# Moving the next image's front work in a four-layer image kernel: statistics among score maxima, filter products in two blocks, and another order of its chain

## What is computed

```python
# L0: decoupled dynamic filter
pooled = x.mean((2, 3))
y = relu(pooled @ w1.T + b1)                       # 12 values
y = (y @ w2.T + b2).reshape(B, C, K * K)           # 9 taps a channel
y = (y - y.mean(-1)) / (y.std(-1, ddof=1) + 1e-10)
cf = y.reshape(B, C * K * K) * fn_std              # channel filter
sf = einsum('bchw,nc->bnhw', x, ws) + bs           # spatial filter, 9 taps a pixel
sf = (sf - sf.mean(taps)) / (sf.std(taps, ddof=1) + 1e-10) * GAIN / K
out = sum over the taps of  patch * cf * sf
# L1: v * sigmoid(q . mean(k))    L2: 3x3 convolution with ternary weights, and bias
# L3: softmax attention over all 3136 pixels: Q, K of 16 channels, V of 64
S = einsum('bkp,bkq->bpq', Q, K)
z = einsum('bpq,bvq->bvp', softmax(S), V)
```

## Time and profile before

| | |
|---|---|
| median of 3 runs | 1789.23 us (1788.2 to 1789.5) |
| profiled execution | 1787.96 us, its span 1786.2 us |
| busy, share of the span | PE 92%, DVE 69%, ACT 68%, POOL 62% |
| mean granted TensorE clock | 0.966 |
| HBM | 8 GB/s over the span |

### The profile page before, as it was taken

The page is one execution under the profiler, slowest core; times in us unless marked ns, Lnnn a source line. Parts: engine busy times, 40 slices in busy tenths (PEclk is TensorE's granted clock), DMA queues, the critical chain, the costliest instruction groups (busy, mean ns, idle before and its releaser), DMA issues.

```text
span 1786.2 us, 29864 instructions
## 1 busy us (share of the span) xinstructions
PE 1635.4 (92%) x10892; PEld 830.9 (47%) x10892; DVE 1239.0 (69%) x2443; ACT 1212.1 (68%) x2300; POOL 1102.3 (62%) x926
## 2 busy tenths in 40 slices
PE   5887899999988799999998979999999888999997
PEld 4464344444446344444443634444444454444442
DVE  5946777775684877777387388777748648777760
ACT  2045899988413689899732378999972337899994
POOL 2720478889751067888865016888887402788888
PEclk9988999999989999999998899999999899999998
DMA  2004000000000400000000040000000012000000
GB/s 88 1 1 90 1 6 7 7 7 6 11 1 1 90 2 6 7 7 12 6 6 1 3 88 1 6 11 7 7 6 6 0 26 29 2 11 7 7 7 11
DMA packets 12388, 26.83 MB, mean 15 GB/s; under 512 B 4560, under 2 KB 8912, under 8 KB 11728
## 3 DMA queue, kind: packets, MB, share of 16 engines
q1 hardware_dynamic: 12240, 24.92, 5.9%
HBM read 8.73 MB, written 6.42 MB: 8 GB/s over the span
## 4 chain that ended last, share of the span: by engine, by line
PE 67%; DVE 17%; ACT 8%; issue 5%; POOL 3%; POOLq 0%; DVEq 0%; ACTq 0%
PE PS L1315 25%; PE PS L1271 12%; PE PS L1241 11%; PE PS L1213 6%; DVE nmt L688 5%; PE PS L1169 3%; ACT Pb L956 3%; DVE nmt L681 3%; DVE Pb L595 3%; ACT PS L911 2%; PE PS L1128 2%; PE PS L1161 2%; PE PS L1204 1%; POOL accP L1076 1%; PE PS L1205 1%
## 5 line engine op out<-in xcount | busy, mean ns | idle before, releaser
L681 DVE TENSOR_REDUCE nmt<-PS 128x1 f32<-128x448 f32 x1176 | 681.2, 618 | 211.5 <-PE PS L1241 207.9
L1076 POOL TENSOR_TENSOR accP<-accP,Pb 128x512 f32<-128x512 f32 (+1 forms) x532 | 677.4, 1273 | 130.3 <-ACT Pb L956 82.2
L956 ACT ACTIVATE Pb<-PS 128x896 f32<-128x896 f32 (+1 forms) x700 | 636.5, 914 | 124.5 <-PE PS L1271 117.2
L1315 PE MATMUL PS<-Pb,VT 128*64 128x448 f32 x2800 | 660.9, 545 | 4.3 <-ACT Pb L956 3.6
L1241 PE MATMUL PS<-Ka,Qa 96*64 96x448 bf16 x2888 | 498.6, 356 | 23.5 <-ACT PS L911 10.7
L1271 PE MATMUL PS<-Qa,Ka 99*64 99x448 bf16 x2744 | 492.4, 354 | 3.0 <-ACT Pb L956 2.5
L911 ACT ACTIVATE PS<-PS,nmt 128x448 f32<-128x448 f32 x588 | 357.1, 607 | 33.6 <-DVE nmt L688 27.9
L1241 PEld LDWEIGHTS PS<-Ka,Qa 96*64 96x64 bf16 x2888 | 166.4, 110 | 269.6 <-issue 116.5
L1271 PEld LDWEIGHTS PS<-Qa,Ka 99*64 99x64 bf16 x2744 | 168.6, 110 | 242.1 <-issue 188.1
L1315 PEld LDWEIGHTS PS<-Pb,VT 128*64 128x64 f32 x2800 | 195.6, 137 | 104.1 <-ACT Pb L956 28.5
L834 ACT ACTIVATE xnp<-xw,nb,rstd 128x448 f32<-128x448 f32 x56 | 40.4, 749 | 195.3 <-DVE nb L503 195.3
(11 more groups left out here) (145 smaller groups left out, 1440.6 us busy)
## 6 DMA issues: line engine op xcount, KB each, us to landing
xin<-in_x SPq DMA_DIRECT2D x4, 1568.0 KB, 11.3
out<-xw SPq DMA_DIRECT2D x28, 224.0 KB, 1.9
Qa<-parts SPq DMA_DIRECT2D x24, 168.0 KB, 7.1
Ka<-parts SPq DMA_DIRECT2D x24, 112.0 KB, 4.0
Ka<-parts SPq DMA_DIRECT2D x24, 84.0 KB, 2.5
Qa<-mpt SPq DMA_DIRECT2D x96, 1.3 KB
wz<-in_weights SPq DMA_DIRECT2D x1, 829.0 KB, 7.7
Qa<-parts SPq DMA_DIRECT2D x24, 28.0 KB, 1.9
```

Of the source, the lines that this page charges most:

```text
L681: nc.vector.reduce_max(nmt[:, target % 2, b, t:t + 1], PS[0:BLK, bank, 0:CH], X, negate=True).then_inc(mx_free, 1)
L956: nc.scalar.activation(Pb[0:r, j % PSLOTS, :, :], PS[0:r, 2 * (k % 2):2 * (k % 2) + 2, 0:CH], ACT.Exp).then_inc(exp_done, 1)
L1076: nc.gpsimd.tensor_tensor((accQ if j < TO_ACCP else accP)[0:r, :, REST:CH], (accQ if j <= TO_ACCP else accP)[0:r, :, REST:CH], Pb[0:r, j % ...
L1315: last = mm(PS[C * h:C * h + C, OB, 0:CH], VT[:, j, C * h:C * h + C], Pb[:, j % PSLOTS, h, :], start=(j == 0), stop=(j == NQ - 1))
```

## The change

The front of the next group begins in superblock 5 and its steps are counted over both superblocks, 0 to 49 (25 is step 0 of superblock 6). The statistics are taken one a step at 3, 5, ... 15, among the last maxima. Mean, variance and power are at 20 to 22, the bias at 23, the normalisations at 24 and 26 to 31, the first layer at 26 and 27. The filter products are in two blocks, sixteen rows' pairs at 30 and twelve at 33. The sums of squares are at 34, the root at 36, the parts at 37, the transposes at 43 to 49, one group a step. The second layer is no longer nine products with a weight column block each: VectorE spreads `y1` over a diagonal mask (`y1d`), one product with `half12` copies it to all partitions (31), and VectorE multiplies it by `w2` (128x108) and sums it over the twelve values (32). POOL's root of the channel filter is at 34, `front_channel_filter` at 35. In the setup the order on VectorE is changed too: `front_centre` and `front_channel_filter` stand ahead of `front_sum_squares` and `front_parts`. The weights lose the block `w2` (1152 columns), the vectors grow from 32 to 152 columns, the constants by 128.

```diff
-FRONT_XN = 7
-FRONT_SF = 8
-FRONT_TR = (20, 20, 21, 22, 23, 24, 24)
-FRONT_ROOT = 16
+FRONT_STATS = (3, 5, 7, 9, 11, 13, 15)
+FRONT_MEAN = 20
+FRONT_XN = (24, 26, 27, 28, 29, 30, 31)
+FRONT_ROWS = {30: (0, 16), 33: (16, 28)}
+FRONT_Y = 31
+FRONT_CF = 35
+FRONT_SQUARES = 33
+FRONT_ROOT = 36
+FRONT_TR = (43, 44, 45, 46, 47, 48, 49)
...
             def front_mid(g):
                 dve.wait_ge(mid_ready, g + 1)
-                nc.vector.tensor_scalar(y1[:, :], front[0:2 * MID, 2:3], v("b1", 2 * MID), 0.0,
-                                        ALU.add, ALU.max).then_inc(y1_ready, 1)
+                link(g, nc.vector.tensor_scalar(y1[:, :], front[0:2 * MID, 2:3], v("b1", 2 * MID), 0.0,
+                                                ALU.add, ALU.max))
+                nc.vector.tensor_scalar(y1d[:, :], v("mask", 2 * MID), y1[:, 0:1], None, ALU.mult).then_inc(y1_ready, 1)
...
                 dve.wait_ge(y_ready, g + 1)
-                link(g, nc.vector.tensor_tensor(yf[:, :], small[:, 8:8 + TAPS], v("b2"), ALU.add))
+                link(g, nc.vector.tensor_tensor(y2[:, :, :], v("w2").rearrange("p (t m) -> p t m", m=MID),
+                                                small[:, 8:8 + MID].unsqueeze(1).to_broadcast([P, TAPS, MID]), ALU.mult))
+                link(g, nc.vector.reduce_sum(ysq[:, :], y2[:, :, :], X))
+                link(g, nc.vector.tensor_tensor(yf[:, :], ysq[:, :], v("b2"), ALU.add))
...
-                    if j == 0:
-                        front_stats(g + 1)
-                    elif j == 3:
+                    if j in FRONT_STATS:
+                        dve.wait_ge(x_loaded, 16 * (g + 2))
+                        last = chunk_stats(xin, FRONT_STATS.index(j))
+                        if j == FRONT_STATS[-1]:
+                            assert n[0] == LINKS, n[0]
+                            n[0] = 0
+                            mean_var(g + 1, 0, last)
+                    elif j == FRONT_MEAN:
                         squares(g + 1, 0, front)
-                    elif j == 4:
                         var_eps(g + 1, 0, front)
-                    elif j == 6:
+                    elif j == FRONT_MEAN + 3:
                         front_bias(g + 1)
-                    elif j == 8:
+                    elif j == NQ + 2:
                         front_mid(g + 1)
-                    elif j == 15:
+                    elif j == FRONT_Y + 1:
+                        front_centre(g + 1)
+                    elif j == FRONT_CF:
+                        front_channel_filter(g + 1)
+                    if j == FRONT_SQUARES + 1:
                         front_sum_squares(g + 1)
-                    elif j == 18:
+                    elif j == FRONT_ROOT + 1:
                         front_parts(g + 1)
-                    elif j == 19:
-                        front_centre(g + 1)
-                    elif j == 22:
-                        front_channel_filter(g + 1)
...
-                        if s == NJ - 1 and more:
-                            front_at(j)
+                        if s >= NJ - 2 and more:
+                            front_at(NQ * (s - NJ + 2) + j)
...
             front_mid(0)
             tap_constants()
+            front_centre(0)
+            front_channel_filter(0)
             front_sum_squares(0)
             front_parts(0)
-            front_centre(0)
-            front_channel_filter(0)
...
-                        if front and j == 5:
+                        if more and s == NJ - 2 and j == FRONT_MEAN + 2:
                             power(g + 1, 0)
-                        if front and j == 21:
+                        if more and s == NJ - 1 and NQ + j == FRONT_Y + 3:
                             channel_root(g + 1)
...
             def front_channel_filter(g):
                 pe.wait_ge(y1_ready, g + 1)
-                for t in range(TAPS):
-                    last = mm(small[:, 8 + t:9 + t], wcol("w2")[0:2 * MID, t * P:(t + 1) * P], y1[:, :],
-                              start=True, stop=True)
-                last.then_inc(y_ready, 1)
-
-            def front_spatial_filter(g, j):
-
-                pe.wait_ge(xn_ready[0], NJ * g + j + 1)
-                for i in range(4 * j, 4 * j + 4):
+                mm(small[:, 8:8 + MID], half12[0:2 * MID, :], y1d[:, :], start=True, stop=True).then_inc(y_ready, 1)
+
+            def filter_rows(g, first, end):
+
+                for i in range(first, end):
+                    if i % 4 == 0:
+                        pe.wait_ge(xn_ready[0], NJ * g + i // 4 + 1)
                     last = mm(PS[0:SP2, SFB, i * PART:(i + 1) * PART], xnp[:, (2 * i + 1) * PW + 1:(2 * i + 3) * PW + 1],
                               wcol("ws"), start=True, stop=True)
-                if j == NJ - 1:
+                if end == NSP:
                     last.then_inc(sfT_ready, 1)
...
-                    if j == 2:
+                    if j == FRONT_MEAN:
+                        pe.wait_ge(mx_free, GROUP_TILES * (g + 1))
+                        pe.wait_ge(mx_summed, GROUP_SUMMED * (g + 1))
                         pair_mean(g + 1, 0, front)
-                    elif j == 3:
+                    elif j == FRONT_MEAN + 1:
                         pair_var(g + 1, 0, front)
-                    elif j == 7:
+                    elif j == NQ + 1:
                         front_mid(g + 1)
-                    elif j == 16:
+                    elif j == FRONT_Y:
                         pe.wait_ge(recip, NJ * g + NJ)
                         front_channel_filter(g + 1)
-                    if FRONT_SF <= j < FRONT_SF + NJ:
-                        front_spatial_filter(g + 1, j - FRONT_SF)
-                    for i in range(NJ):
-                        if FRONT_TR[i] == j:
-                            front_transpose(g + 1, i)
+                    if j in FRONT_ROWS:
+                        filter_rows(g + 1, *FRONT_ROWS[j])
+                    if j in FRONT_TR:
+                        front_transpose(g + 1, FRONT_TR.index(j))
...
             front_mid(0)
-            for j in range(NJ):
-                front_spatial_filter(0, j)
+            filter_rows(0, 0, NSP)
             front_channel_filter(0)
```

More of the change, by code:

```diff
@@ L1056, in scale_sums, with superblock @@
                     nc.gpsimd.tensor_tensor(sme[:, :, :], sm[:, s % 2, :, :], ef[:, :, :], ALU.mult).then_inc(dstep, 1)
-                def superblock(sidx, s, first, front=False):
+                def superblock(sidx, s, first):
                     for j in range(1, NQ):
```

47 lines of the change are left out of this document (24 added, 23 removed).

## The result

The changed kernel takes 1797.9 us (median of 11 runs, 1787.31 to 1803.22) against 1789.23 (11 runs, 1787.65 to 1790.5); the ratio is 1.0043 [1.0024 to 1.0063]. Forecast were 1794.8 and slower. Two numbers matter beside the median. The runs of the kernel before lie within 3 us, those of the changed kernel over 16. And the time follows the mean granted TensorE clock of the run: 0.969 in the run of 1787.31, 0.963 in that of 1795.2, 0.958 in that of 1803.22; over the eleven runs the correlation is -0.98. Where the clock holds, the changed kernel is as fast as the kernel before or faster; mostly it doesn't hold.

The account below looks back on a forecast made before the run. POOL was taken to set the last superblock's pace once PE fills the buffers. Three groups losing 0.7 us (1.9 clock less 1.2 gained), 2.1, plus setup 3.4 gave +5.5 on 1787.96: 1793.5, median 1794.8, range 1783 to 1802.

Parts of the forecast that it names:

- Setup: VectorE's centre and channel filter ahead of the setup's sums of squares: 3.4 us lost once, bounds 2.9 and 4.2.
- Superblock 5: Statistics among the maxima at odd steps, later small matmuls hidden: 0.1 us lost a group, bounds 0 and 0.5.
- The two starvations: Last superblock: POOL waits 2.4 us at sum 8 behind the first block, 2.2 at sum 12 behind the root.
- Group without the clock: Superblocks 5 and 6 of a group, before any price for a lowered clock: 1.2 us gained.
- Clock: TensorE's clock falls in or behind the first block: 1.9 us lost a group, bounds 0 and 5.
- Rival 3: Low clock over both blocks and the steps between, 5 us a group: 9.3 us more, 1804; chance 0.10.
- rival 1: Clock holds in the blocks; groups win 3.6 us, the setup loses 3.4: 1789.0; chance 0.25.
- Rival 2: Blocks don't starve POOL, as with faster packed products: 1781.8, or 1775 without the root's starvation too; chance 0.15.
- Rival 5: The setup's cost is hidden by something unseen: 1791.4; chance 0.04.
- Tables: Table switches at the spatial filter's root: exponential 1.29 us behind the load by trace, against the page's 2.66 a switch.
- rival 4: The page's price of table switches at the root holds: 8 us more, 1803; chance 0.02.
- Transposes: From step 18 of the last superblock, PE doesn't wait for VectorE's parts, with about 1.3 us to spare.

Follow-up runs that it names:

- both repairs: Changed kernel with VectorE's old setup order and the filter products in seven groups of four at steps 27 to 33: 1788.67 us, ratio 0.9995 to the kernel before.
- version with small groups: Changed kernel with its filter products in seven groups of four at steps 27 to 33 instead of two blocks: 1792.19 us, ratio 1.0025 to before.
- version with only the first block: Changed kernel with the sixteen-row block kept and the twelve-row one split into fours at steps 31 to 33: 1797.59 us, ratio 1.005 to before.

## Why the prediction was right, and where it wasn't

The sign, the place (a clock that falls behind the first block, and the setup) and the range were right; the sum was 3.1 us short, and it was an average over two cases that are 5 to 8 us apart.

- **Setup.** 3.4 forecast, 3.8 in the traces (sums of squares at 33.07 where I had 32.6, first tap at 46.28 where I had 45.9), and 3.8 at the first tap when undone. Each new operation took 0.27 (0.3 taken). Right; the rest is spread over the chain.
- **Superblock 5.** The step that failed. I took 0.1 us a group with 0.5 as its bound; it is 1.57, and my own mark (over 0.5) is passed. Two things were missed. At step 15 the last statistic has the aggregation of 0.34 and the column sums beside it, and the maximum comes late: step 17 is 2.06 instead of 1.58. Steps 18 to 21 give a quarter of that back. And steps 22, 23 and 24, where I called the small matmuls and the first normalisation hidden, take 1.60, 1.59 and 1.47 instead of 1.14, 1.21 and 1.15: two products of 0.38 us stand ahead of PE's scores, and 0.75 us of normalisation ahead of ScalarE's exponential. That is 1.16 of the 1.57. The statistics at the odd steps before 15 cost under 0.1 together, as taken. The reason I gave, POOL's backlog, did hold for half: POOL's sum 1, counted from superblock 5's first exponential, is 0.74 us later (41.14 against 40.40), where I had 0.5 with the power. So a term that was missed by 1.5 us cost 0.24.
- **The two starvations.** 2.4 and 2.2 us forecast at sums 8 and 12; 2.65 and 1.75 in group 0. Sums 5 and 7 have small waits besides; in groups 1 and 2 there is a third long one, 5.67 at sum 11, which came with the low clock and which I had excluded (none else over 0.7). From sum 1 to the last one's end are 42.5 us where I had 41.9. Right.
- **Group without the clock.** -1.2 forecast; from superblock 5's first exponential to POOL's last sum 83.62 (83.46 in the version with the setup undone) against 84.00 in group 1 of the kernel before, which I had priced, so -0.4 to -0.5. (Its group 0 took 84.76.) The gain was over-estimated by the 0.24 and the 0.6 (42.5 less 41.9) of the two points above.
- **Clock.** 1.9 us a group as a mean, bounds 0 and 5. Of the profiled groups one lost none of it in the blocks, two lost 5.4 against the kernel before and 5.6 against the first. The quarter of a stretch for the other places was about right: group 0 fell once at the root, and its tap is 86.15 against 85.74 in the version where it didn't fall. My working had one stretch of 3.3 us; it was 13.65, and 17.1 in other versions. I priced a fall by the kernel before, where dense work follows it, and didn't ask what follows here. Rival 3 had this mechanism (low over both blocks and the steps between, 1804) with a chance of 0.10, and rival 1 the other (it holds, 1789.0) with 0.25. That the forecast lies near the median is in part luck: it priced a mean that none of the profiled groups has, 1.9 us where the groups have 0.4 or 5.4. The fastest runs, 1787.31 and 1788.74, are at rival 1, the slowest, 1802.34 and 1803.22, at rival 3, and the median is between. Treating the clock as one number was the mistake of form: in the profiled groups of the changed kernel it is one or the other. The last superblock was to take 43 to 46 us; it took 42.5, 47.2 and 47.3. The median, less the setup's 3.8, leaves (1797.9-1789.2-3.8)/3 = 1.6 us a group, where I had 0.7.
- **Rival 2** (blocks don't starve POOL) fell: 3.43 us for 32 matmuls is 0.107 each, 0.115 was taken. **Rival 5** fell with the setup undone.
- **Tables.** The exponential began 1.30 us behind its load (899.49 to 900.79), as in the earlier trace rows. The Trainium skill ("ScalarE: Activation LUTs", What ACT_TABLE_LOAD costs) gives 2.66 us with a drain; the measurement decides against it, and rival 4 falls.
- **Transposes** didn't wait: VectorE's parts end at 908.4 in group 1, the first transpose starts at 910.18. There the forecast left 1.3 us and 1.8 were left, with everything later.
- **Where the expected gain went.** After both repairs the time equals the kernel before. By the version with small groups POOL starves for 1.16 us once, 0.93 three times and 1.92 at sum 12 instead of 0.69, 0.93 and 3.84, and 0.74 us are lost on the way to sum 1. The 12 us of front were moved, not hidden.

**What stays open.** Why the clock falls in one group and not in the next of the same kernel, with the same instructions before it: only the group's place in the run differs. The falls of superblocks 5 and 6 are a part of all: the traces (the one with the root on POOL apart) have the clock low for 115 to 150 us, in the setup, the taps and the layers between as well, and these stretches shift from version to version (124.6 us in all before, 141.6 after), so that one profiled run and another differ by more than superblocks 5 and 6. And what exactly made the difference between the channel product between the blocks and behind them: the edit moved the product, VectorE's channel filter and POOL's root of it together, and each version has one trace. Where the product or filter products followed the fall directly, the clock stayed low for 13.7 to 17.1 us in a piece; where plain steps followed, for 3.4 to 6.8. But the second falls of the version with the product behind the blocks have it in them and lasted 6.8. That thin matmuls keep the clock low is thus my reading, and was not tested by itself.

## What to carry to other kernels

Price a lowered TensorE clock by what stands behind the place where it falls, and as a case that happens or not, not as a mean: the same block cost nothing, 1.7 or 5 to 8 us a group, in versions that differ in what followed it. Leaving dense steps only between long thin matmuls, with the small product behind them, gave the fastest version here; try it, although the cause isn't isolated. If work is moved ahead within one engine's order, look also at the places where it runs once without cover, such as a setup: 3.8 us here, nearly half of the whole loss.

## What the runs showed of the hardware

- The clock fell to 1.2 GHz behind or inside 32 matmuls of 18 columns (3.43 us, 4.20 and 4.28 where it fell inside), with PE busy throughout, in some groups and not in others. With the same matmuls in eights between steps it stayed at 2.4 GHz in all three groups of the trace. In the version with only the first block such eights ran at the low clock, 1.73 us each, and it didn't come back until behind them.
- PE was busy for all of the 13.65 and the 17.07 us at 1.2 GHz; no idle time was needed for that.
- POOL's power costs 0.55 us on one column and 9.30 on 56, where its addition of 512 columns takes 1.27.
- VectorE's operations beside POOL's sums: casting 504 columns took 1.38 us against 0.42 in the setup, a multiplication of 56 columns by a number 1.16 against 0.19. The Trainium skill ("GPSIMD Engine Reference", Specifications) has the two share their way to the memory when VectorE reads two tensors or works in a mode with two ports; these are operations with one input tensor, so by the page it would be the mode, and the traces don't show which mode they ran in.
